# Second attention of a two-layer transformer: where the next group's query preparation stands, and value products in one run

## What is computed

```
q = rmsnorm(hidden_states @ wq_a.T, q_a_ln_w) @ wq_b.T
q_nope, q_pe = (q[..., :NOPE], q[..., NOPE:])
q_pe = apply_rope(q_pe, cos, sin)
q_abs = jnp.einsum('bhsd,hdc->bhsc', q_nope, q_absorb)
scores = (einsum('bhsc,btc->bhst', q_abs, kv) + einsum('bhsd,bxtd->bhst', q_pe, k_pe)) * SCALE
attn = softmax(where(causal, scores, min), axis=-1)
x = jnp.einsum('bhst,btc->bhsc', attn, kv)
```

## Time and profile before

| | before |
|---|---|
| median of 3 runs | 1603.35 us (1600.1 to 1606.49) |
| the profiled execution | 1605.04 us |
| its span | 1603.5 us |
| TensorE busy | 1262.6 us (79%) |
| VectorE busy | 895.1 us (56%) |
| ScalarE busy | 734.5 us (46%) |
| GpSimd busy | 520.2 us (32%) |

### The profile page before, as it was taken

The page is one execution under the profiler, slowest core; times in us unless marked ns, Lnnn a source line. Parts: engine busy times, 40 slices in busy tenths (PEclk is TensorE's granted clock), DMA queues, the critical chain, the costliest instruction groups (busy, mean ns, idle before and its releaser), DMA issues. The chain is left out here.

```text
span 1603.5 us, 22609 instructions
## 1 busy us (share of the span) xinstructions
PE 1262.6 (79%) x7428; PEld 893.8 (56%) x7428; DVE 895.1 (56%) x2331; ACT 734.5 (46%) x1668; POOL 520.2 (32%) x556
## 2 busy tenths in 40 slices
PE   2675729888888838677699999997575999999977
PEld 1564714433333317466576666765564677777656
DVE  6656538766666533343666666661243666666640
ACT  1544403555454620452566666650153666666640
POOL 0221233333233110040355555530050555555520
PEclk8797955888777968788899999998797999999998
DMA  2213187554453049301111111005102111111005
GB/s 78 109 60 123 56 99 64 55 59 58 51 59 37 22 153 269 112 2 63 47 37 37 37 37 37 27 14 158 49 1 85 25 39 38 39 39 39 18 28 157
DMA packets 133157, 101.02 MB, mean 63 GB/s; under 512 B 48240, under 2 KB 120368, under 8 KB 132784
## 3 DMA queue, kind: packets, MB, share of 16 engines
q1 hardware_dynamic: 132000, 98.53, 27.4%
q10 hardware_dynamic: 1040, 1.05, 0.2%
HBM read 56.30 MB, written 34.87 MB: 57 GB/s over the span
## 5 line engine op out<-in xcount | busy, mean ns | idle before, releaser
L748 POOL TENSOR_SCALAR a_p<-a_p,a_rl 128x128 f32<-128x128 f32 (+7 forms) x256 | 215.6, 842 | 400.1 <-DVE a_rl L690 400.1
L731 ACT ACTIVATE a_p<-psum,a_nm 128x128 f32<-128x128 f32 (+7 forms) x256 | 189.5, 740 | 107.5 <-DVE a_nm L684 106.9
L1225 ACT ACTIVATE a_pt<-psum 128x512 f32<-128x512 f32 (+3 forms) x384 | 166.9, 492 | 154.3 <-PE psum L1098 152.8
L1088 PE MATMUL psum<-a_op_k,a_op_q 64*128 64x512 f32 (+3 forms) x384 | 162.6, 510 | 52.9 <-POOL a_op_k L1023 32.1
L781 PE MATMUL psum<-ident,a_p 128*128 128x128 f32 x1152 | 170.1, 275 | 31.8 <-DVE a_pt L717 31.8
L803 PE MATMUL psum<-a_pt,v 128*64 128x256 f32 (+1 forms) x1280 | 158.9, 370 | 1.1 <-ACT a_ot L817 1.1
L781 PEld LDWEIGHTS psum<-ident,a_p 128*128 128x128 f32 x1152 | 129.6, 140 | 53.5 <-issue 48.3
L684 DVE CUSTOM_DVE_ANT_0 psum<-psum,mask_a 128x128 f32<-128x128 f32 (+3 forms) x128 | 63.8, 499 | 149.4 <-PE psum L766 149.3
L1098 PE MATMUL psum<-a_op_q,a_op_k 64*128 64x512 f32 (+3 forms) x384 | 134.7, 455 | 0.0
L715 ACT ACTIVATE a_pt<-psum 128x256 f32<-128x256 f32 (+2 forms) x192 | 87.4, 455 | 94.8 <-PE psum L781 93.8
L1088 PEld LDWEIGHTS psum<-a_op_k,a_op_q 64*128 64x128 f32 x384 | 79.6, 235 | 90.3 <-issue 32.3
(11 more groups left out here) (257 smaller groups left out, 2810.7 us busy)
## 6 DMA issues: line engine op xcount, KB each, us to landing
a_swap<-a_raw SPq DMA_DIRECT2D x64, 128.0 KB, 2.3
ot_d<-a_ot SPq DMA_DIRECT2D x16, 512.0 KB, 2.6
o_ot<-ot_d SPq DMA_DIRECT2D x16, 512.0 KB, 6.2
a_raw_q<-qk_d SPq DMA_DIRECT2D x48, 128.0 KB, 5.1
a_raw_k<-qk_d SPq DMA_DIRECT2D x48, 128.0 KB, 9.5
a_wf<-wf_d SPq DMA_DIRECT2D x16, 384.0 KB, 3.2
qk_d<-p_stage_h SPq DMA_DIRECT2D x8, 512.0 KB, 2.7
qk_d<-p_stage_l SPq DMA_DIRECT2D x8, 512.0 KB, 3.4
```

The source lines that it names most:

```text
L731: e.activation(s.p[:, t % NPB, 0:(i + 1) * P], C.score[t % 2][:, 0:(i + 1) * P], ACT.Exp, scale=-1.0, bias=s.nm[:, k:k + 1], accum_out=s.l ...
L748: e.tensor_scalar(s.p[:, t % NPB, 0:(i + 1) * P], s.p[:, t % NPB, 0:(i + 1) * P], s.rl[:, k:k + 1], 1.0, ALU.mult, ALU.mult).then_inc(s.no ...
L1088: e.matmul(bank_a("score", g, k)[:, 0:k1 - k0], q[rows(hd), hd % 2, i * P:(i + 1) * P], kk[rows(hd), hd % 2, k0:k1], start=True, stop=True ...
L1225: e.activation(pt[:, k // G0 % NPT, hd, off:HALF], bank_b("score", g, k)[:, off:HALF], ACT.Exp, scale=-1.0).then_inc(exped, 1)
```

## The change

The value product of a chunk is issued in one run, 6 steps after the chunk's last (`pieces` = 1), and its output is copied out one step later. The rotary rows are exchanged, rotated, copied and reduced to their remainder in two halves of 512 tokens for both heads, instead of one head at a time over 1024. All four tables have lower steps.

```
-        self.pieces = self.per_chunk - 1
+        self.pieces = 1
...
             else:
-                hd = k - 4
-                r = PE_ROWS[hd]
-                e.wait_ge(roped, g * 6 + 6)
-                e.activation(q[u][hd][0][r, :], raw[r, :], ACT.Copy).then_inc(qhi, 1)
+                half = k - 4
+                t = slice(half * HALF, (half + 1) * HALF)
+                e.wait_ge(roped, g * 6 + 3 * half + 3)
+                for hd in range(2):
+                    r = PE_ROWS[hd]
+                    e.activation(q[u][hd][0][r, t], raw[r, t], ACT.Copy).then_inc(qhi, 1)
...
         def prep_dve(e, g, u, k):
...
+            e.wait_ge(qhi, g * 8 + 2 * (k - 1))
+            half = k % 2
+            t = slice(half * HALF, (half + 1) * HALF)
+            for hd in range(2):
+                if k < 4:
                     r = LAT_ROWS[hd]
+                    whole = place(g, k)[r, :]
+                else:
+                    r = PE_ROWS[hd]
+                    whole = raw[r, t]
+                e.tensor_tensor(q[u][hd][1][r, t], whole, q[u][hd][0][r, t].bitcast(F32), ALU.subtract).then_inc(qlo, 1)
...
-        AT_PE = {0: 0, 2: 1, 4: 2, 6: 3}
-        AT_ACT = {0: 0, 2: 1, 4: 2, 6: 3, 12: 4, 13: 5}
+        AT_PE = {0: 0, 1: 1, 3: 2, 5: 3}
+        AT_ACT = {0: 0, 1: 1, 3: 2, 5: 3, 6: 4, 9: 5}
...
-                    e.wait_ge(raw_out, (g + 1) * 2)
-                    for r in range(0, P, 64):
-                        e.dma_start(swap[r:r + 32, :], raw[r + 32:r + 64, :]).then_inc(swapped, 16)
-                        e.dma_start(swap[r + 32:r + 64, :], raw[r:r + 32, :]).then_inc(swapped, 16)
+                    for half in range(2):
+                        t = slice(half * HALF, (half + 1) * HALF)
+                        e.wait_ge(raw_out, 2 * g + half + 1)
+                        for r in range(0, P, 64):
+                            e.dma_start(swap[r:r + 32, t], raw[r + 32:r + 64, t]).then_inc(swapped[half], 16)
+                            e.dma_start(swap[r + 32:r + 64, t], raw[r:r + 32, t]).then_inc(swapped[half], 16)
```

More of the change, by code:

```diff
@@ L1726, in attend1 @@
         raw_out = ph.sem("raw_out")
-        swapped = ph.sem("swapped")
+        swapped = [ph.sem("swapped0"), ph.sem("swapped1")]
         roped = ph.sem("roped")
@@ L1744, in prep_pe @@
                 if later:
-                    e.wait_ge(qlo, g * 6)
+                    e.wait_ge(qlo, g * 8)
             elif not later:
@@ L1750, in prep_pe @@
             else:
-                e.wait_ge(qhi, g * 6 + 2)
-                e.wait_ge(qlo, g * 6 + 2)
+                e.wait_ge(qhi, g * 8 + 2)
+                e.wait_ge(qlo, g * 8 + 2)
             c = k % 2
@@ L1767, in prep_act @@
                 if later and k == 0:
-                    e.wait_ge(qhi, g * 6)
-                    e.wait_ge(qlo, g * 6)
+                    e.wait_ge(qhi, g * 8)
+                    e.wait_ge(qlo, g * 8)
                 t = slice(k * HALF, (k + 1) * HALF)
@@ L1778, in prep_act @@
             else:
-                hd = k - 4
-                r = PE_ROWS[hd]
-                e.wait_ge(roped, g * 6 + 6)
-                e.activation(q[u][hd][0][r, :], raw[r, :], ACT.Copy).then_inc(qhi, 1)
-        def prep_dve(e, g, u, k):
-            if k < 4:
-                e.wait_ge(qhi, g * 6 + 2 * (k - 1))
-                t = slice((k - 2) * HALF, (k - 1) * HALF)
-                for hd in range(2):
-                    r = LAT_ROWS[hd]
-                    e.tensor_tensor(q[u][hd][1][r, t], place(g, k)[r, :], q[u][hd][0][r, t].bitcast(F32),
-                                    ALU.subtract).then_inc(qlo, 1)
-            else:
-                hd = k - 4
-                r = PE_ROWS[hd]
-                e.wait_ge(qhi, g * 6 + 5 + hd)
-                e.tensor_tensor(q[u][hd][1][r, :], raw[r, :], q[u][hd][0][r, :].bitcast(F32),
-                                ALU.subtract).then_inc(qlo, 1)
+                half = k - 4
@@ L1800, in rotate @@
         def rotate(e, g, k):
-            t = slice((k % 2) * HALF, (k % 2 + 1) * HALF)
-            if k < 2:
-                e.wait_ge(swapped, (g + 1) * 64)
+            half, part = k // 3, k % 3
+            t = slice(half * HALF, (half + 1) * HALF)
+            if part == 0:
+                e.wait_ge(swapped[half], (g + 1) * 64)
                 e.tensor_tensor(swap[:, t], swap[:, t], st[:, t], ALU.mult).then_inc(roped, 1)
-            elif k < 4:
-                e.wait_ge(raw_out, g * 2 + 2)
+            elif part == 1:
+                e.wait_ge(raw_out, g * 2 + half + 1)
@@ L1877, in slot @@
                         g = t // PREP
-                        e.wait_ge(qhi, (n * 2 + g + 1) * 6)
-                        e.wait_ge(qlo, (n * 2 + g + 1) * 6)
+                        e.wait_ge(qhi, (n * 2 + g + 1) * 8)
+                        e.wait_ge(qlo, (n * 2 + g + 1) * 8)
                     softmax_pe(e, C, s, n, t, later, score, value, KL)
```

4 lines of the change are left out of this document (2 added, 2 removed).

## The result

| | before | after |
|---|---|---|
| median (lowest to highest) | 1604.9 us (1600.1 to 1609.4) | 1641.0 us (1633.0 to 1646.9) |
| profiled execution: time, span | 1605.0, 1603.5 us | 1646.9, 1645.3 us |
| mean granted clock of TensorE | 0.874 | 0.869 |

The ratio of the runs is 1.0222, with a 95% interval of 1.0165 to 1.0279: 36 us slower. I had forecast 1624 (range 1598 to 1638). The direction and most of the mechanism came as told; the time lies just above the range.

The account below looks back on a forecast made before the run. TensorE's queue was taken as the bound. Twelve groups at plus 1.7 us (20.4), first groups plus 5.0, prologue, last groups and tail minus 4.2 gave plus 21.2 on the median 1603.35: 1624 us, range 1598 to 1638.

Parts of the forecast that it names:

- The pieces: TensorE's value products: each piece left out saves about 0.3 us, six per group, 1.8 us if TensorE stays the bound.
- The exchange: Rotary rows: eight DMAs, half as large, instead of four; landed within 2.3 us before GpSimd needs them, counted as nothing.
- The walk: Queues followed from P(3)'s end to S(13): score waits of 4.25 us instead of 0.35, S(5) to S(13) plus 3.0.
- What the halves cost: Rotary remainders and copies: half a remainder 0.70 us, whole 1.22; per group 0.3 us more on VectorE, 0.26 on ScalarE.
- The third rival, the clock: Steps 6 to 9: granted clock falls to 1.2 GHz after the new waits; 70 us on top, 1694; chance 0.03.
- The first groups: First group of each batch: no old value products to save, same walk behind P(3); plus 2.5 us, twice, 5.0.
- The rest of the program: Prologue, last group and tail of each batch: together 4.2 us saved.
- The prologue: Before a batch's S(0): last copy and remainder overlap by halves; minus 0.8 us, twice.
- last group and tail: End of each batch: last group minus 0.8 us, as it prepares nothing; tail minus 0.5, saving two pieces; each twice.
- The first rival: Second attention's groups: TensorE stays the bound and the moved work lies in slack; 1565 us; chance 0.12.
- the second (no change): Score waits in the groups are a half to two thirds as long; 1595 to 1605 us; chance 0.11.
- the wait above 1 us at T(12): Sign in a steady group: TensorE still waits above 1 us at T(12) for VectorE's evacuation of a transpose bank.

Follow-up runs that it names:

- one_run_only: The kernel before with each chunk's value product in one run and nothing else changed; 1605.0 us, ratio 1.001.
- after_no_scale: The changed kernel with GpSimd's scaling of the probabilities cut to one column; 1626.4 us.
- halves_old_steps: The changed kernel's halves of the rotary rows, but with the old step tables and value products in three pieces as before; 1628.3 us, ratio 1.015.
- low_one_run: The kernel before with lower steps, rotary rows still whole, and value products in one run; 1630.4 us, ratio 1.019.
- the fills: Idle matmuls added in TensorE's waits, in the changed kernel (1638.3 us) and in the kernel before with one value run per chunk (1596.4 us).

## Why the forecast was right and wrong

**The pieces: right.** Value runs have one gap each, and six switches are worth 1.8 us per group. one_run_only saves only 0.65, because T(11) waits 1.39, and S(9) and S(11) come about 0.3 and 0.2 later behind the scores before them; T(10) and T(12) give 1.0 back against the earlier trace rows. That makes 0.9; the other 0.25 is not accounted for.

**The exchange: right.** Its DMAs land in 2.0 us for 64 KB each (2.3 for 128 in the earlier trace rows), and nothing waits for them. The kernel with lower steps and whole rows, whose exchange is the old one, shows the same waits at S(8) and S(9) (0.70 and 0.80).

**The walk: right up to S(9), and late from the first remainders of the rotary rows on.** Times from P(3)'s end (874.79 in the change):

| | S(8) | S(9) | S(10) | S(11) | S(12) | S(13) |
|---|---|---|---|---|---|---|
| forecast | 2.5 | 4.7 | 7.25 | 9.05 | 11.4 | 14.4 |
| trace | 2.44 | 4.84 | 7.73 | 9.50 | 11.85 | 15.29 |
| after_no_scale | 2.43 | 4.82 | 7.44 | 9.20 | 11.55 | 14.63 |

S(13) to the next S(0) takes 8.21 (forecast 9.04 - 0.8 = 8.24), S(0) to S(5) 12.94 (13.17). The whole excess, 0.9, arises ahead of two places. The k=4 pair of remainders ends at 5.71 instead of 5.15: it starts 0.28 late, since copy and maximum of step 7 take longer than I had them, and is 0.27 longer. The k=5 pair ends at 12.55 instead of 11.65: it starts 0.54 late, mostly by what is behind already, and is 0.36 longer. So 0.6 of the 0.9 is the length of the remainders, and leaving out the scaling takes 0.66 off at S(13).

**The step that failed is "What the halves cost", the price of a remainder's half from SBUF.** I bounded it by 0.61 and 0.70 and took 0.70. That is its length alone (0.69); beside GpSimd it is 0.96 to 1.33, in halves_old_steps 1.50. The upper bound came from remainders that read PSUM (0.66 to 0.70 in every run), and the two kinds differ in just this. The rows to see it by were in the trace of before: GpSimd's 1.91 us for a scaling beside L1797. I counted the rotation as six GpSimd instructions kept, as if GpSimd's queue touched nobody's. It is worth 0.64 of the 0.68 us by which a group at full clock missed: 42.17 against the 41.49 forecast, 41.53 without the scaling. That the rest comes out at nearly nothing is partly luck: S(13) is 0.2 late even without the scaling, and S(0) to S(5) is 0.2 shorter than forecast. Whole rows with one run give 41.46, but their copies and remainders stand in other steps, so this is no test of the walk. 12 x 0.68 = 8.2 us.

**The third rival, the clock, was no rival but a part.** I gave it 3% at 70 us. The clock did fall, in four of twelve groups, at S(9), after S(8) and S(9) had waited 0.7 and 0.8, and each fall costs 0.8: 3.2 us in the profiled execution. My reason, that the steady loop of before keeps 1.00 over waits of 1.3, did not carry over: one_run_only's waits of 1.39 and 0.92, one step apart, bring it to 0.70. How long a single wait is doesn't decide, and neither do the two waits: low_one_run and after_no_scale have the same ones (0.70 and 0.80) and stay at 1.00. The Trainium skill ("TensorE: Matmul & The Clock Gate", part 1) gates the clock by how busy TensorE has been recently; the fills agree, which add work and keep 1.00, but they shorten the waits too and so can't tell the two apart.

**The first groups: 7.9 instead of 5.0.** That is 4.0 and 3.9 each. With whole rows at the lower steps they are already 3.7 and 3.4 longer, with one run on top 3.1 and 3.8; leaving out the scaling takes 0.5 off the change's. So the steps alone are enough, and little of it is GpSimd; halves at the old steps cost 2.4 and 2.2 there. Which wait I left out is not settled. **The rest of the program: plus 1.6 instead of minus 4.2.** The prologue gave its 0.8 in each batch (17.59 to 16.82 from the first projection to S(0)); last group and tail lost 0.4 in each batch where I had them gain 1.3; 3.2 lie ahead of anything changed.

Added up for the profiled executions: forecast 21.2; plus 8.2 (period at full clock, nearly all of it the remainders beside GpSimd), 3.2 (clock), 0.5 (the two groups of 42.4), 2.9 (first groups), 5.8 (rest) is 41.8. The halves' price is the largest single miss in the mechanism, but alone it would have given about 1632 us, inside the range; the clock, the first groups and the rest took the median to 1641.

**The first rival (TensorE stays the bound) and the second (no change) were refuted**: the waits ahead of S(8) to S(13) are 3.97 us, where the first needed less than 2.7. Of the signs that I named, the wait above 1 us at T(12) did not come: it is 0.94.

## What to carry to other kernels

Before splitting an instruction, look at what it reads and at who works beside it. A VectorE operation on two SBUF tensors that starts ahead of GpSimd's scaling ran its own time here (1.20 us). Cut in two it let GpSimd in between (the second half took 1.50 instead of 0.69), which turned a split that costs nothing by itself into 1.5 us per group. A switch saved on the busiest engine is a gain only as far as the piece that goes wasn't covering something; price the cover as well as the piece. And where waits of about a microsecond stand close together, read the granted clock of the stretch behind them, compare periods at equal clock, and try idle matmuls in the waits: they turned a change worth nothing into 0.5%.
